# Zero products behind every gathered tile in a graph network kernel, and one bank fewer in a ring

## The reference

```python
# L0, three layers
h = jnp.einsum('ni,rio->nro', x, weight)          # weight from bases and comp
msg = h[src, etype]
cnt = segment_sum(ones, dst * R + etype)          # R = 8
norm = 1.0 / jnp.maximum(cnt[seg], 1.0)
agg = segment_sum(msg * norm[:, None], dst)
x = agg + x @ root_l + bias_l                     # batch norm and relu between layers
# L1, three hops
cur = segment_sum(cur[col] * edge_weight[:, None], row)
acc = acc + cur
```

## Time and profile before

| | |
|---|---|
| median of three runs | 8715.2 us |
| profiled execution | 8786.1 us, of which the span from the first to the last instruction is 8784.4 us |
| mean granted clock of PE | 0.769 of 2.4 GHz |
| busy PE / DVE / POOL | 5157.0 / 4103.6 / 6015.8 us |
| gathers | 2490 in the layers, 2418 in the hops |
| float32 product records | 4980 in the layers, 4836 in the hops |

### The profile page before, as it was taken

One profiled execution on the slowest core, in us unless ns is written; L12 is line 12 of the kernel. 1 busy time (PEld: TensorE's weight loads), 2 busy tenths in 40 slices (PEclk: granted clock), 3 DMA queues, 4 the chain that ended last, 5 costly groups with the idle time before them and its releaser, 6 DMA issues.

```text
span 8784.4 us, 72860 instructions
## 1 busy us (share of the span) xinstructions
PE 5157.0 (59%) x14185; PEld 2298.0 (26%) x14185; DVE 4103.6 (47%) x10640; ACT 678.5 (8%) x1792; POOL 6015.8 (68%) x5938
## 2 busy tenths in 40 slices
PE   5800066776735455554555557667667767677776
PEld 2300044444423333323333321111111112111111
DVE  8910044444424444424444455545555545555556
ACT  4900000000200000010000010000000000000000
POOL 3877766666776666676666647777677777677674
PEclk8955577777867766776767679888888888888888
DMA  4000011111411111141111111111101111211111
GB/s 148 5 5 1 4 45 45 45 45 45 129 40 47 46 47 46 42 130 46 46 46 46 46 37 23 23 23 23 29 23 23 23 23 23 36 23 23 23 23 31
DMA packets 239208, 346.49 MB, mean 39 GB/s; under 512 B 129619, under 2 KB 138878, under 8 KB 238706
## 3 DMA queue, kind: packets, MB, share of 16 engines
q0 software_dynamic: 182992, 245.38, 12.9%
q1 hardware_dynamic: 55712, 96.16, 3.3%
q10 hardware_dynamic: 130, 0.80, 0.0%
HBM read 253.24 MB, written 87.84 MB: 39 GB/s over the span
## 4 chain that ended last, share of the span: by engine, by line
PE 34%; issue 19%; another core or an unknown queue 17%; POOL 16%; DVE 11%; DMA 2%; DVEq 1%; ACT 0%; POOLq 0%; SPq 0%
PE psum L860 22%; POOL placed_src L489 11%; PE psum L822 10%; POOL msg L516 3%; DVE agg_and L1229 3%; DVE sel L1206 2%; PE psum L758 2%; DMA msg<-hop_table,stage_idx 1%; POOL msg L505 1%; DVEq L1229 1%; DVE bufD L1216 1%; DVE sel L1253 1%; DVE agg_and L1261 1%; DVE sel L1203 1%
## 5 line engine op out<-in xcount | busy, mean ns | idle before, releaser
L516 POOL DMA_INDIRECT msg<-hop_table,stage_idx x2418 | 2496.8, 1033 | 1107.8 <-issue 621.8
L505 POOL DMA_INDIRECT msg<-msg_table,visit_src x2490 | 2435.5, 978 | 1173.0 <-issue 628.1
L860 PE MATMUL psum<-sel,msg 128*64 128x512 f32 x4836 | 2482.9, 662 | 1043.6 <-issue 769.9
L822 PE MATMUL psum<-sel,msg 128*128 128x256 f32 x4980 | 1781.2, 516 | 1955.1 <-DVE agg_and L1229 832.6
L822 PEld LDWEIGHTS psum<-sel,msg 128*128 128x128 f32 x4980 | 1203.5, 257 | 2459.1 <-issue 1233.6
L1229 DVE TENSOR_TENSOR agg_and<-agg_and,psum 128x256 f32 x1245 | 523.5, 420 | 2441.9 <-PE psum L822 1169.3
L1261 DVE TENSOR_TENSOR agg_and<-agg_and,psum 64x512 f32 x1209 | 818.3, 677 | 1693.4 <-remote 823.7
L860 PEld LDWEIGHTS psum<-sel,msg 128*64 128x64 f32 x4836 | 662.9, 148 | 2861.6 <-issue 2318.8
L489 POOL DMA_INDIRECT placed_src<-stage_pay,stage_addr x800 | 1024.9, 1281 | 304.7 <-issue 216.3
L1253 DVE TENSOR_SCALAR sel<-iota,agg_and 128x512 f32<-128x512 f32 x2418 | 1096.2, 492 | 0.1
L1206 DVE TENSOR_SCALAR sel<-iota,agg_and 128x256 f32<-128x256 f32 x1660 | 593.2, 421 | 12.9 <-ACT agg_and L621 12.6
(11 more groups left out here) (201 smaller groups left out, 1730.2 us busy)
## 6 DMA issues: line engine op xcount, KB each, us to landing
msg_table<-sel SPq DMA_DIRECT2D x147, 512.0 KB
msg<-msg_table,visit_src POOLq DMA_INDIRECT x2490
msg<-hop_table,stage_idx POOLq DMA_INDIRECT x2418
placed_src<-stage_pay,stage_addr POOLq DMA_INDIRECT x800
hop_table<-sel SPq DMA_DIRECT2D x21, 224.0 KB, 3.1
bufE<-inv_sqrt SPq DMA_DIRECT2D x2, 1568.0 KB, 10.2
out<-cur SPq DMA_DIRECT2D x12, 256.0 KB
placed_src<-sel SPq DMA_DIRECT2D x1, 806.0 KB, 6.8
```

The lines of the kernel that those rows point to most:

```text
L505: g.indirect_dma_start(out=msg[:, n % MV, :], out_offset=None, in_=msg_table, in_offset=bass.IndirectOffsetOnAxis(ap=visit_src[:, v:v + 1] ...
L516: g.indirect_dma_start(out=msg[:, b, 0:H], out_offset=None, in_=hop_table, in_offset=bass.IndirectOffsetOnAxis(ap=stage_idx[:, b:b + 1], a ...
L822: t.matmul(psum[:, banks[c % len(banks)], at:at + W2], msg[:, n % MV, :], visit_sel[:, n % SV, :], start=v % 2 == 0, stop=v % 2 == 1).then ...
L860: t.matmul(psum[0:H, b // 2 % PB, :], msg[:, b, 0:H], sel[:, b % SB, :], start=b % 2 == 0, stop=b % 2 == 1).then_inc(summed, 1)
```

## The change

`SPREAD` loses bank 6 and keeps 2 and 3. Bank 6 becomes `SPARE`. A new function `keep_warm(bank, times)` on PE multiplies a block of zeros, 128 x 128 in float16, by zeros of 512 columns, and writes the result into that bank; nothing reads it, it waits for nothing and signals nothing. It is called after every product of a visit, twice in the first layer and three times in the other two (`FILL`), and once after every product of a hop. These are 830 x 8 + 2418 = 9058 products more, each with its weight load.

```diff
-SPREAD = (2, 3, 6)
+SPREAD = (2, 3)
+SPARE = 6
+FILL = (2, 3, 3)
...
+            def keep_warm(bank, times):
+
+                for _ in range(times):
+                    t.matmul(psum[:, bank, :], zeros16[:, 0:128], zeros16[:, :], start=True, stop=True)
+
...
                         t.matmul(psum[:, banks[c % len(banks)], at:at + W2], msg[:, n % MV, :], visit_sel[:, n % SV, :],
                                  start=v % 2 == 0, stop=v % 2 == 1).then_inc(visit_summed, 1)
+                        keep_warm(SPARE, FILL[k])
...
                         t.matmul(psum[0:H, b // 2 % PB, :], msg[:, b, 0:H], sel[:, b % SB, :],
                                  start=b % 2 == 0, stop=b % 2 == 1).then_inc(summed, 1)
+                        keep_warm(SPARE, 1)
```

## The result

| | before | after |
|---|---|---|
| median of the runs, us | 8713.4 (8704.8 to 8729.6, 4 runs) | 8838.1 (8827.6 to 8853.4, 4 runs) |
| profiled execution, us | 8786.1 | 8853.4 |
| granted clock, mean | 0.769 | 0.899 |
| PE busy, us | 5157 | 7013 |
| POOL's waits in the six stages, us | 674 | 697 |

The last row is the idle time between gathers less 0.304 us for each, the step from one gather to the next, and less the waits for a table. The prediction has the same sum for the kernel before with 0.30 us: 696.

A forecast was written before the change was run, and what follows sets the result against it. The bound was a loop with POOL slowest, waiting 696 us for late PE reports. Gains of 416 us (layers 2, 3, hops) and 123 us (layer 1) took 8715 to 8176, stated as 8175; range 8030 to 8590.

The forecast's parts named there:

- What bounds the kernel: In the six stages: a loop whose slowest member is POOL, able to go at 1.27 to 1.34 us per gather.
- The 696 us: POOL's waiting in three layers and three hops, 696 us together, all put down to PE reporting late.
- Why PE is late: In the stages, a product's report can arrive many us after its record when PE falls idle; 696 us at stake.
- the case built on it: Rival: late reports have a cause apart from PE's idling, so DVE's waits stay; 8620 to 8750 us, chance 0.10.
- The clock: PE's granted clock, 0.70 to 0.87 in the profiled stages, was to reach 0.95 or more in all six.
- The price of a block: Each product of zeros on PE: 0.22 us at the high clock, 0.43 at the low; upper price 0.32.
- The ring: Two banks for layer 1's spreads: harmless while reports are prompt; bounds there 176 us gained to 50 lost.
- the cover of 1.5 us: Layer 1's slack per two chunks: loop of 8.7 us against POOL's 10.2; without it each late us costs one.
- The gain of 123 us in layer 1: 70% of POOL's 175.8 us of waiting in layer 1, expected to go.
- The sum: Over all six stages: 416 us from layers 2, 3 and hops plus 123 from layer 1, 539 us gained.
- The clock rises and nothing follows: Rival for the stages: DVE's waits stay and only faster catching up is gained; 8620 to 8750 us, chance 0.10.
- Slower: blocks are load: Rival, layers 2 and 3 first: blocks load PE without raising its clock, below 0.80; about 9180 us, chance 0.06.

The follow-up runs named there:

- e5_before: The kernel before the change, unedited, run again in a later session: 8076.5 us, ratio 0.9997.
- e3_apart: Kernel before, products reading the identity instead of gathered messages, POOL waiting only for its own earlier gathers, not for PE: 11417.7 us, ratio 1.299.
- e6_after: The changed kernel, unedited, in a session where the kernel before took 8080.2 us: 8045.3 us, ratio 0.9957.
- e2_tiny: The changed kernel with as many blocks of zeros, each 16 columns wide instead of 512: 8916.3 us, ratio 1.0141 to the kernel before.
- e1_ring: The kernel before with only SPREAD cut to banks 2 and 3, no blocks of zeros: 8792.2 us, ratio 1.0000.
- e14_paced: The kernel before with a small fill on POOL ahead of each gather of layers and hops: 8727.8 us, ratio 1.0016.
- e4_loop: The kernel before with PE's code of each hop as a loop on the engine, not written out: 8811.4 us, ratio 1.0024.
- e13_16bit: The kernel before with message products taking only the upper 16 bits of each value, in one pass: 8675.4 us, ratio 0.9954.
- e18_apart: Kernel before, products reading the identity instead of gathered messages, so POOL never waits for PE; second run, another session: 11437.4 us, ratio 1.2974.
- e8_paced: The kernel before with a small fill on POOL ahead of each gather, in a session with before at 8080.2 us: ratio 1.0035.

## Why the prediction was wrong

*What bounds the kernel: half right.* The loop's slowest member is POOL, and its pace of 1.27 to 1.34 us was read rightly: e5_before runs at 1.277 in the layers and 1.331 in the hops. The 696 us were also about the right size for what the waits cost: where they are absent before takes 8080 us, 635 under its first median.

*Why PE is late: here the prediction failed.* It said that a report "can arrive many us after its record when PE falls idle". I had read it from PE's 14.9 us of idle time behind a late report; but idling is not the cause. The changed kernel keeps PE busy 93% of hop 1, and POOL's waits in the six stages are 697 us for 674. e3_apart shows the late reports tied to POOL's gathers, e5_before shows them gone with nothing changed in the program. I had the observation against me in my own text (products kept starting from 2541 to 2549.6 while DVE already waited) and gave the case built on it 0.10.

*The clock: right, a little high.* "0.95 or more" came as 0.92 in the layers and 0.96 to 0.97 in the hops late, 0.99 to 1.00 on time. I had weighed that zeros might be work that does not lift the clock. They are not: in layer 2 e6_after has it at 1.00 with blocks of zeros and e5_before 0.63 without. The Trainium skill, "TensorE: Matmul & The Clock Gate", Part 4, says that a transpose does not count as busy in the same way; no run here tests a transpose.

*The price of a block: right in the layers, mis-sized in the hops.* 0.22 us taken; 0.22 measured in layer 2 with three in a row, 0.46 between tiles of a hop. The difference cost nothing that can be measured: e2_tiny, with blocks of 16 columns, loses the same.

*The ring.* Alone it costs 0 us (e1_ring). I had feared that each us of a late report would cost a us once the cover of 1.5 us was gone; the reports were late in that session, and layer 1 took 1234.4 us for 1235.0, though without blocks. With blocks the ring was not run apart; layer 1 of the changed kernel took 3 us more than before. The gain of 123 us in layer 1 failed with the reports, not with the ring.

*The sum.* 539 us of gain were all from the failed step; nothing of them came. In their place stands a term that I did not have: 18,116 instructions of TensorE at 6.9 ns, 125 us. Why an instruction costs that is open.

*The rivals.* "The clock rises and nothing follows" is what the profile shows, but it was priced at 8620 to 8750 because I saw no way for it to be slower. "Slower: blocks are load" had the sign, and the wrong mechanism: its condition was a clock below 0.80. None of the cases held 8838.

*What stays open.* What holds PE's reports, and why in some sessions only. The trace has the symptom (late only from PE, while POOL issues and some 25 us longer, more for each instruction of PE) but no record of the path. Whether it is POOL's issuing or the traffic of its gathers was not separated, and stops of POOL were not tested (e14_paced has none). Fetching is excluded (e4_loop), PE's load (e2_tiny) and its idling (the changed kernel). The Trainium skill, "NOTIFIC — the notification-queue block", section 7.1, says that the block which takes the engines' event records holds the engines up when its inner pipeline fills, and does not drop records. A price per instruction whatever its length would fit that; no run here shows it. A profiled execution takes no longer than the others of its session (8791.8 us against a median of 8792.2 in e1_ring), but that does not speak against it, since a span and a granted clock are on record for every execution, and so each may have been recorded. One thing in the traces points to the recording: while gathers flow, the profile of before lists 3,279 updates for 6,388 instructions of DVE that make one, and e5_before 6,419 for 6,421. In the late profile half of them are missing, on time almost none. Whether records were lost, which would not go with that section, or were never made the traces do not tell. So the recording itself may be what makes a session late; that is a rival which no run here tests.

No version that ran beats both kernels at both levels: the changed kernel wins 0.4% on time and loses 1.4% late, e13_16bit wins 0.5% late, at the price of half the bits.

## What to carry to other kernels

When one engine waits for a count that another's records say is complete, the loss can be on the way of the report; find first what else is going on at the time (here gathers on GpSimd), and do not take the idle time that follows for the cause. Raise an engine's clock only if that engine sets the pace: here 0.63 to 1.00 brought 1.8 us in a stage of 1065. Added instructions can have a price per piece apart from their time, so test them at almost no length, and measure a small change in more than one session, since this one changed its sign. And look that an edit makes the stop or the load it is meant to make: the fills here vanished in a gap that was there anyway.

## What the runs showed of the hardware

- One program took 8080 or 8790 us in two sessions with the same chip number, with nearly the same instruction lengths; each session was steady within 0.5%.
- In the late sessions, with GpSimd issuing gathers back to back, a PE report reached DVE 29 us late in the hops, and 0.15 us after the record once that was over (e3_apart, e18_apart).
- TensorE instructions, added or taken away, changed the time by 4 to 7 ns each in those sessions, whether they ran 16 columns, 512, or were a loop's own; in the on-time ones 18,116 of 16 columns changed it by 1.6 us, within the noise.
- A single float16 product of 512 columns between float32 ones of 512 lengthened the tile by 0.46 us at the high clock; three in a row between float32 ones of 256 took 0.22 us each.
- A fill of 0.12 us on GpSimd between two gathers did not lengthen the 0.30 us that lie between them (e8_paced, e14_paced).
- Products of zeros lift the granted clock: 0.63 to 1.00 in layer 2 (e5_before, e6_after).
